# Moving the expert result stores of a two-layer MoE kernel from ScalarE's queue to SyncE's

## The reference, cut to what matters

```python
x = x + 0.5 * _L0_ffn_ref(_layernorm(x), ...)
x = x + _L0_attn_ref(_layernorm(x), ...)
x = x + 0.5 * _L0_ffn_ref(_layernorm(x), ...)
x = x + 0.5 * _L1_ffn_ref(_layernorm(x), ...)      # MoE, called m3 in the kernel
x = x + _L1_attn_ref(_layernorm(x), ...)           # linear attention
x = x + 0.5 * _L1_ffn_ref(_layernorm(x), ...)      # MoE, called m5

# _L1_ffn_ref: 16 experts, top 2 of each token
logits = x_flat @ Wr + br
topk_w, topk_idx = top_k(softmax(logits), 2)        # weights divided by their sum
h = layernorm(einsum('nc,ech->neh', x_flat, W1) + b1, g1, be1)
expert_out = einsum('neh,eho->neo', gelu(h), W2) + b2
y_flat = sum(take(expert_out, topk_idx) * topk_w)
```

## Time and profile before

| | us |
|---|---|
| median of 3 runs | 696.82 |
| lowest and highest run | 694.99, 805.44 |
| span of the profiled execution | 603.3 |

### The profile page before, as it was taken

One profiled execution on the slowest core, in us unless ns is written; L12 is line 12 of the kernel. 1 busy time (PEld: TensorE's weight loads), 2 busy tenths in 40 slices (PEclk: granted clock), 3 DMA queues, 4 the chain that ended last, 5 costly groups with the idle time before them and its releaser, 6 DMA issues.

```text
span 603.3 us, 9389 instructions
## 1 busy us (share of the span) xinstructions
PE 495.1 (82%) x3064; PEld 269.9 (45%) x3072; DVE 461.9 (77%) x1226; ACT 313.2 (52%) x613; POOL 164.0 (27%) x206
## 2 busy tenths in 40 slices
PE   6786989999999999899787899597896787799800
PEld 3452422222222222244365788485654454688600
DVE  4988898988878987465897889668877766978822
ACT  2354456777776678687142677444341101567700
POOL 5020030010000110001374604672101074711765
PEclk8898999999999999999888899878897888899955
DMA  6006400049705003000326295411000015273532
GB/s 208 3 6 162 90 2 0 21 110 193 247 2 141 3 9 63 2 1 1 118 87 166 81 310 152 135 36 28 1 0 1 2 52 140 76 221 88 156 104 65
DMA packets 55773, 49.48 MB, mean 82 GB/s; under 512 B 5406, under 2 KB 47918, under 8 KB 55342
## 3 DMA queue, kind: packets, MB, share of 16 engines
q1 hardware_dynamic: 34974, 31.21, 19.3%
q0 software_dynamic: 4368, 9.54, 5.9%
q10 hardware_dynamic: 16384, 8.13, 4.8%
HBM read 25.90 MB, written 20.60 MB: 77 GB/s over the span
## 4 chain that ended last, share of the span: by engine, by line
PE 48%; DVE 26%; POOL 8%; issue 7%; ACT 6%; DMA 3%; SPq 0%; POOLq 0%; ACTq 0%; DVEq 0%
PE ps L819 9%; DVE arena L867 8%; PE ps L809 7%; PE ps L766 7%; POOL arena L1198 5%; PE ps L1287 3%; PE ps L1260 3%; POOL rows_in L1171 2%; PE ps L1586 2%; ACT arena L1357 2%; PE ps L207 1%; PE ps L1243 1%; PE ps L1270 1%; PE ps L1642 1%; DMA row<-in_rows 1%
## 5 line engine op out<-in xcount | busy, mean ns | idle before, releaser
L867 DVE TENSOR_REDUCE arena<-ps 128x1 f32<-128x1024 f32 x128 | 150.8, 1219 | 25.1 <-PE ps L766 24.8
L932 ACT ACTIVATE arena<-ps 128x512 f32<-128x512 f32 x256 | 138.4, 602 | 55.2 <-PE ps L809 52.9
L809 PE MATMUL ps<-arena 99*128 99x512 bf16 x256 | 85.5, 383 | 1.2 <-ACT arena L932 1.0
L766 PE MATMUL ps<-arena 96*128 96x512 bf16 x256 | 76.6, 381 | 7.0 <-DVE arena L867 6.7
L1198 POOL DMA_INDIRECT arena<-rows_out,route x64 | 61.2, 957 | 68.9 <-DMA rows_out<-arena 47.7
L1171 POOL DMA_INDIRECT rows_in<-xl,route x64 | 62.5, 977 | 53.3 <-DVE route L1123 35.1
L819 PE MATMUL ps<-arena 128*32 128x512 f32 x512 | 68.2, 605 | 1.9 <-ACT arena L928 1.3
L809 PEld LDWEIGHTS ps<-arena 99*128 99x128 bf16 x256 | 22.3, 97 | 73.0 <-ACT arena L932 48.8
L254 POOL TENSOR_TENSOR small<-small,nhalf 128x8 f32<-128x8 f32 x11 | 18.2, 1656 | 121.3 <-DVE small L276 121.3
L1357 ACT ACTIVATE arena<-ps,route 128x128 f32<-128x128 f32 x124 | 46.4, 461 | 5.2 <-PE ps L1270 5.1
L207 PE MATMUL ps<-zerob 128*128 128x512 bf16 x140 | 41.3, 446 | 2.5 <-POOL zerob L2101 1.4
(11 more groups left out here) (280 smaller groups left out, 825.9 us busy)
## 6 DMA issues: line engine op xcount, KB each, us to landing
arena<-rows_in SPq DMA_DIRECT2D x28, 256.0 KB, 4.3
rows_out<-arena ACTq DMA_DIRECT2D x28, 256.0 KB, 2.9
rows_in<-zerob SPq DMA_DIRECT2D x2, 1920.0 KB, 11.0
arena<-att_parts SPq DMA_DIRECT2D x12, 256.0 KB, 8.7
arena<-in_consts SPq DMA_DIRECT2D x2, 1024.0 KB, 6.7
arena<-zerob SPq DMA_DIRECT2D x1, 2048.0 KB, 10.1
arena<-att_parts SPq DMA_DIRECT2D x14, 128.0 KB, 8.1
att_parts<-arena SPq DMA_DIRECT2D x6, 256.0 KB
```

The costliest lines, as they stand in the source:

```text
L766: ins = pe.matmul(ps[:, bank + keys, :], a_qs[0:96, b, h, j * P:(j + 1) * P], a_ks[0:96, b, h, keys * 512:(keys + 1) * 512], start=True, s ...
L809: pe.matmul(ps[:, score_bank(n), :], a_ks[0:99, b, h0 + h4, i * P:(i + 1) * P], a_qs[0:99, b, h0 + h4, half * 512:(half + 1) * 512], start ...
L867: nc.vector.tensor_reduce(a_nm[:, o % 2, k:k + 1], ps[:, bank:bank + 2, :].rearrange("p a b -> p (a b)"), AX.X, ALU.max, negate=True).then ...
L932: nc.scalar.activation(a_p[:, n % 16, :], ps[:, score_bank(n), :], ACT.Exp, scale=0.25).then_inc(a.ex, 1)
```

## The change

The store's DMA, its wait for `t.yc` and its semaphore stay as they are, but SP issues it. In SP's list the 16 stores of a layer stand behind all 16 loads of the layer, and in m3 also behind the 2048 KB clear of `l_vp`. The ACT list loses all its `store` steps.

```diff
-        def moe_scalar_store(act, m, g):
+        def moe_sync_store(sp, m, g):
             b, u = m.b, NGR * m.i + g
-            act.wait_ge(t.yc, u + 1)
+            sp.wait_ge(t.yc, u + 1)
             k = tiles_in(g)
-            act.dma_start(rows_out[b].rearrange("(j p) c -> p j c", p=P)[:, 4 * g:4 * g + k, :],
+            sp.dma_start(rows_out[b].rearrange("(j p) c -> p j c", p=P)[:, 4 * g:4 * g + k, :],
                           t_y[:, u % 4, 0:k, :]).then_inc(t.ys[u % 4], 16)
...
+        def moe_sync_stores(sp, pair):
+            for m in pair:
+                for g in range(NGR):
+                    moe_sync_store(sp, m, g)
...
-            def store(u):
-                moe_scalar_store(act, pair[(u - u0) // NGR], (u - u0) % NGR)
-
             for u in range(u0, last - LEAD):
-                if u >= u0 + 2:
-                    store(u - 2)
                 if u + LEAD + 1 < last and u + LEAD + 1 != u0 + NGR:
                     rows(u + LEAD + 1)
                 gelu(u)
...
             out_in(last - 4)
-            store(last - 5)
             gelu(last - 3)
-            store(last - 4)
             gelu(last - 2)
             out_in(last - 3)
             gelu(last - 1)
-            store(last - 3)
             out_in(last - 2)
-            store(last - 2)
             out_in(last - 1)
-            store(last - 1)
...
             moe_sync(sp, m3)
             sp.dma_start(l_vp.rearrange("p t h d -> p (t h d)").rearrange("p (a b) -> p a b", b=256),
                          bc(zerof[:, :].unsqueeze(1), [P, 16, 256])).then_inc(l.clear, 16)
+            moe_sync_stores(sp, m3)
             moe_sync(sp, m5)
+            moe_sync_stores(sp, m5)
```

## The result

| | us |
|---|---|
| before, median of 7 runs | 694.99 |
| changed kernel, median of 7 runs | 699.27 |
| ratio, 95% interval | 1.0082 (1.0060 to 1.0105) |
| span of the profiled execution | 697.1 (its own time 698.95) |

The medians are of all seven executions and lie 4.3 us apart, while the ratio leaves out one far slower execution of each kernel (805.44 and 1197.36 us). By the ratio the change costs 5.7 us (0.0082 x 695), and the interval excludes zero. It is slower, by less than 2%, and inside the forecast range. A second measurement on another occasion gave 1.0069 (1.0041 to 1.0097), 4.8 us.

What follows compares the result with a forecast made beforehand. PE was busiest (82% of a 603.3 us span), but the chain runs through store(7) and POOL's gathers, so late stores count one for one. +6.3 +2.5 -0.6 = +8.2 us on 696.8 gives 705.0 us, range 697.5 to 712.

Steps and rivals of the forecast that it cites:

- out_in(4) starting [late] and waiting for the DMA rows_out<-arena: Expected sign in m3: ACT's out_in(4) starts at 361 to 364 us, waiting for store(0) to land.
- if the gathers of m3 start less than 5 us later: Sign of being wrong: POOL's m3 gathers less than 5 us later; first gather was forecast at about 376.5 instead of 368.0.
- Part 1: 32 store issues leave ACT's queue in m3 and m5; only m5's chain piece counts: -0.6 us, ends 0 and -11.7.
- The rival built on it: Stall in m3 hidden or short, only ACT's 0.6 us gained: 696.2 us; chance 0.15 for neutral or short stall together.
- The rival of a half stall: m3's stall only half as long, clock kept: 699.7 us; chance 0.15 for neutral or short stall together.
- Part 2: m3's stores 0 to 3 wait behind loads and clear; out_in(4) 7.2 us late, out(5) 6.3 us late: +6.3 us.
- Part 3: PE's clock falls to about half after idling some 6 us in m3, slowing the PE-bound work behind: +2.5 us.
- Part 4: m5's stores stand behind loads only and land before out_in(20) needs them: 0 us, ends 0 and +3.
- The sum: Whole kernel: +6.3 (out(5) late) + 2.5 (clock) - 0.6 (ACT) = +8.2 us, 705.0 us, 1.2% more.
- What lies around it (93.5 us) stays: Time outside the profiled 603.3 us span taken as fixed at 93.5 us, so +8.2 was added to the 696.8 median.

Runs made afterwards that it cites:

- doubled clear: Changed kernel with a second 2048 KB transfer of zeros behind the clear and ahead of m3's stores; ratio 1.0139 to the kernel before.
- m5 alone: Kernel before with only m5's stores issued by SP, m3's staying on ACT; ratio 0.9999.
- the kernel with the clear behind: Changed kernel with the 2048 KB clear moved behind m3's stores; ratios to the kernel before 0.9994 and, measured again, 0.9999.
- twelve copies: Kernel before, stores on ACT, with twelve spare 128x128 copies on ACT ahead of out_in(4) in m3; ratio 1.0050.
- m3 alone: Kernel before with only m3's stores issued by SP, behind loads and clear, m5's staying on ACT; ratio 1.0040.
- the clear early: Changed kernel with the clear issued between the loads of m3's two halves, while SP waits for half 1's scatters; ratio to the kernel before 0.9993.
- before again: Kernel before, unchanged, run for a second profile; ratio 1.0007, span 693.2 us.
- four and twelve copies: Kernel before with four or twelve spare 128x128 copies on ACT ahead of out_in(4) in m3; ratios 1.0003 and 1.0050.

## Why the prediction was right, and where it was not

**The mechanism** of the wait stands: "out_in(4) starting [late] and waiting for the DMA rows_out<-arena", since store(0) is behind loads and clear. The doubled clear makes it longer, and each way of taking the clear away removes the loss (0.9991 to 0.9999 four times, 1.0005 with the clear on ACT's queue). But one of the prediction's own signs of being wrong came true: "if the gathers of m3 start less than 5 us later". They start 1.1 us later behind out_in(3), and 3.9 us later from the start of the span (396.82 and 392.88). What was predicted is the right wait in the right place, but a stall of 6 to 8 us with a fall of the clock, and that is not what happened.

**Part 1**, -0.6 us for ACT's issues: too small to see, and m5 alone (0.9999) fits it. Of the rule in the Trainium skill, "DMA: Bandwidth & Descriptors", section "Issuing engines are not separate DMA queues", that the choice only saves sequencer time, this case shows the half that matters here: with the clear out of the way the choice is worth nothing either way. The rival built on it (696.2, no stall) is the result of the kernel with the clear behind, not of the change. The rival of a half stall (699.7) comes nearest to the 699.27 measured, but also by luck: it had 3.5 us of direct delay, not 1.1.

**Part 2 failed in size.** The term was "out_in(4) is then 7.2 us late", and the wait is 1.5; out(5) was to be 6.3 late, and it is 0.75 late behind out_in(3) (7.26 us against 6.51). The first gather is 1.0 to 1.1 late. Two errors:
- When the clear is issued relative to out_in(4): 1.5 us ahead in the first profile, 8.85 in the usual execution, because there the engines have stood still during POOL's scatters: out_in(0) starts at 366.4, behind the last scatter of half 1 (355.57), and in the first profile at 339.9, ahead of it (343.47). This is the large one.
- When store(0) lands behind the clear's issue: forecast 362.3 - 353.5 = 8.8 us, measured 374.77 + 9.65 - 374.02 = 10.4. The DMA engines moved less than I had put (345 GB/s): 261 in the view of 374 to 383.5 us, which holds the start, and 289 in the three us from 377.02 on:

```profile
DMA packets 2834, 2.48 MB, mean 261 GB/s; under 512 B 34, under 2 KB 2834, under 8 KB 2834
...
arena<-zerob SPq DMA_DIRECT2D x1, 2048.0 KB, 9.5
```

With the forecast's 8.8 and the usual 8.85 there would have been no wait at all.

A reading of part 2 goes too far as well: that stores on ACT's queue would not share the time with the clear. The earlier trace rows ends at 360, and from about 360.2 on the two queues share packet by packet.

**Part 3**, +2.5 us for the clock: not in the changed kernel right behind its stall, where the clock stays at 1.00; PE's pause there is 0.76 us, and the pauses ahead of the stretches of the earlier trace rows were 2.3. Its reasoning fits the stall that I had in mind: the doubled clear pays about 3.5.

**Part 4**, nothing in m5: right (0.9999).

**The sum.** "What lies around it (93.5 us) stays" was the step that let all this pass. A span 92 us shorter than the median is not a fixed cost around the span but another execution; 1.85 us lie around. I had the two numbers side by side and explained the gap away. So +8.2 against +5.7 is partly luck: the direct term is 1.1, and the rest is something that I had not in the sum.

**What stays open** is that rest. Why does 1.1 us at the first gather cost 4.8 to 5.7 at the end, and 1.66 from spare copies 3.5, while 0.25 costs nothing that can be seen and 10.0 (doubled clear) costs 9.6, not more? It is not proportional. The executions of the changed kernel are also more spread, 697.8 to 704.1 in its first measurement, and before mostly 692.5 to 696.8. Longer executions mostly have the lower mean clock: with twelve copies the three shortest are at 0.861 to 0.866 and the three longest, from 702.55 us on, at 0.850 to 0.853; of the changed kernel 703.69 and 704.13 us are at 0.848 and 697.77 at 0.857, though 698.95 is at 0.845. The profile of m3 alone, a 699.25 us execution, spends 96.6 us from its second half's first gather in m3 to the first scatter in m5, where the others spend 89 to 93. This points to TensorE's clock behind the later standstills, whose timing a small shift may change. It is not shown: before and the clear early have a long time from g0 to out_in(15) in the table with no loss in their ratio, and the twelve copies a short one with a loss. One profile of a kernel can't settle a distribution.

## What to carry to other kernels

Moving a store to another queue is a question of what stands ahead of it in the new list and how long the buffer it empties can wait. Here a store has about 9 us from the place of the clear until its buffer is wanted, a 2048 KB transfer in front uses 10.4, and half of it is free. The wait of 1.5 us that is left cost about 5 us of time, so a short stall should be measured and not added up. And compare the profile's span with the median of the runs before reading a single row: here 1.8 to 2.1 us lie around the span in every execution for which time and span are both known, and a profile with 92 between it and the median was of another kind of execution. Relative timing between engines taken from such a one misleads, even where every single duration is right.

## What the runs showed of the hardware that was not expected

- In the usual execution ACT and DVE stand still for 4 to 15 us at a time while POOL issues indirect DMAs (before: the waits without a named source of 4.40, 15.52, 3.94, 4.92 and 7.58 us in m3's chain; such waits are 13% of the whole chain). The two longest end 3.5 and 3.8 us behind the start of the last indirect DMA, the others while POOL is still issuing. In one profiled execution of the same program they did not, and it was some 90 us shorter. What they wait for no view names, and it was not tried.
- A 256 KB store that is issued behind a 2048 KB clear lands in some 7 to 10 us instead of 2.1 to 2.7, on the clear's queue or on the other. On the other queue it moves nothing for 4.3 to 4.8 us from its issue, and then the two queues move the same number of packets. "DMA: Bandwidth & Descriptors" of the Trainium skill, section "Queues, rings and completion order", has an engine go round the queues that have work: the second part of these stretches shows it (230 and 229 packets from 377 to 378 with the clear on ACT's queue), the first (959 and none from 373.2 to 376) does not.
- The 2048 KB clear, with no other queue moving, went at 288 to 291 GB/s from SP's queue in five profiles (before again, changed twice, m3 alone, doubled clear), at 297 to 314 in three more (m5 alone, four and twelve copies), at 346 in the first profile of before, and at 354 from ACT's queue. Why it differs was not tried.
- Twelve copies of 128x128 from PSUM took 0.18 us each back to back, where four Gelus of this size in a row take 0.38 each (1.50 us for the four in the timelines).
